# Context attention in a two-layer decoder: from four-head groups in steps to a stream of head pairs

## What is computed

```python
x = x + _L0_xattn_ref(_layernorm(x, axis=-1), ctx_1024, ctx_1024, mask, Wq, bq, Wk, bk, Wv, bv, Wo, bo)

def _L0_xattn_ref(query, key, value, mask, ...):      # 16 heads of 16 features
    q, k, v = proj(query, Wq, bq), proj(key, Wk, bk), proj(value, Wv, bv)
    scores = einsum('bhqd,bhkd->bhqk', q, k) / sqrt(16)
    scores = where(mask == 0, -1e9, scores)            # layer 0 only
    p_attn = softmax(scores, axis=-1)
    return einsum('bhqk,bhkd->bhqd', p_attn, v) ... @ Wo.T + bo
```

## Time and profile before

| what | value |
|---|---|
| median of 3 runs | 2990.66 us |
| lowest and highest | 2989.32 and 2998.60 us |
| profiled execution, its own time | 2986.54 us |
| its span in the profile | 2984.9 us |
| mean granted TensorE clock | 0.886 |

### The profile page before, as it was taken

One profiled execution on the slowest core, in us unless ns is written; L12 is line 12 of the kernel. 1 busy time (PEld: TensorE's weight loads), 2 busy tenths in 40 slices (PEclk: granted clock), 3 DMA queues, 4 the chain that ended last, 5 costly groups with the idle time before them and its releaser, 6 DMA issues. The chain is left out here.

```text
span 2984.9 us, 46600 instructions
## 1 busy us (share of the span) xinstructions
PE 2419.0 (81%) x15980; PEld 1321.5 (44%) x15980; DVE 1588.0 (53%) x2548; ACT 1155.4 (39%) x2075; POOL 984.6 (33%) x836
## 2 busy tenths in 40 slices
PE   3748996575899697799999998858739999847996
PEld 3613434234788475233333332733512222246885
DVE  2758873437233332666666663233658999553223
ACT  1516664242000232344444444224416777711221
POOL 0831003301222111576777776130560000003331
PEclk7959998576999898899999999866869999968998
DMA  3442212432564576122222221543451121024555
GB/s 110 100 89 59 59 38 67 80 72 90 168 211 159 180 195 188 51 77 83 86 77 84 82 78 42 155 73 71 109 102 55 31 57 34 8 76 154 197 195 175
DMA packets 250865, 299.71 MB, mean 100 GB/s; under 512 B 64174, under 2 KB 196948, under 8 KB 250196
## 3 DMA queue, kind: packets, MB, share of 16 engines
q1 hardware_dynamic: 221684, 227.59, 26.2%
q0 software_dynamic: 27104, 68.49, 8.6%
q10 hardware_dynamic: 1920, 1.57, 0.3%
HBM read 205.49 MB, written 91.25 MB: 99 GB/s over the span
## 5 line engine op out<-in xcount | busy, mean ns | idle before, releaser
L1749 ACT ACTIVATE a_probs<-a_cols 128x512 f32<-128x512 f32 (+3 forms) x896 | 445.2, 549 | 239.1 <-PE a_cols L1680 162.1
L1770 DVE TENSOR_REDUCE a_mxw<-a_rows 128x2 f32<-128x1024 f32 (+1 forms) x448 | 475.4, 1099 | 70.6 <-PE a_rows L1638 42.3
L2196 DVE TENSOR_REDUCE a_mxw<-a_rows 128x2 f32<-128x1024 f32 x256 | 313.3, 1224 | 208.3 <-PE a_rows L2034 206.6
L2174 ACT ACTIVATE a_probs<-a_cols 128x1024 f32<-128x1024 f32 x256 | 261.9, 1025 | 266.7 <-PE a_cols L2063 249.6
L2015 POOL TENSOR_TENSOR a_sums<-a_sums,a_probs 128x1024 f32<-128x1024 f32 x128 | 309.6, 2419 | 100.3 <-ACT a_probs L2174 87.1
L1680 PE MATMUL a_cols<-a_qs,a_ks 50*128 50x512 bf16 (+7 forms) x1792 | 275.4, 363 | 17.6 <-DMA a_qs<-a_nparts 11.5
L2450 PE MATMUL e_psU<-e_xT,e_w 128*128 128x256 f32 x1216 | 273.8, 384 | 1.9 <-ACT e_xT L2497 1.2
L2059 PE MATMUL a_cols<-a_qf,a_kf 64*128 64x512 f32 x1024 | 266.5, 598 | 0.0
L522 PE MATMUL t_psP<-t_xT,t_wf 128*128 128x256 f32 x1024 | 236.6, 389 | 36.7 <-ACT t_xT L615 18.1
L1638 PE MATMUL a_rows<-a_ks,a_qs 48*128 48x512 bf16 (+3 forms) x896 | 174.3, 385 | 111.9 <-DMA a_ks<-k_scratch 68.1
L1708 PE MATMUL a_out<-a_probs,a_vs 128*17 128x256 f32 (+4 forms) x3328 | 255.6, 380 | 0.2 <-ACT a_probs L1749 0.2
(11 more groups left out here) (248 smaller groups left out, 3045.7 us busy)
## 6 DMA issues: line engine op xcount, KB each, us to landing
e_w<-in_w SPq DMA_DIRECT2D x69, 512.0 KB
e_w<-in_w SPq DMA_DIRECT2D x30, 1024.0 KB
qk_wide_scratch<-t_f SPq DMA_DIRECT2D x32, 512.0 KB, 2.9
q_scratch<-t_parts POOLq DMA_DIRECT2D x128, 96.0 KB, 2.4
a_qs<-q_scratch SPq DMA_DIRECT2D x96, 128.0 KB
a_qs<-q_scratch SPq DMA_DIRECT2D x168, 64.0 KB, 2.3
a_ks<-k_scratch SPq DMA_DIRECT2D x144, 64.0 KB, 2.6
vw_scratch<-t_v SPq DMA_DIRECT2D x16, 520.0 KB, 7.2
```

Source lines behind the costliest of these rows:

```text
L1749: act.activation(pr[ug % RING][:, 2 * hp + e, c0:512], psC[(2 * at + e) % 3][:, 0:512 - c0], ACT.Exp, scale=scale).then_inc(ex_done, 1)
L1770: dve.tensor_reduce(mxw[w][:, a, :, hp, t % 4:t % 4 + 1], src[:, :, 0:n], AX.X, ALU.max).then_inc(s_free, 1)
L2174: act.activation(pr[i][:], psC[i % 2][:], ACT.Exp, scale=scale).then_inc(ex_done, 1)
L2196: dve.tensor_reduce(mxw[:, j % 2, :, j // 2:j // 2 + 1], psR[:], AX.X, ALU.max).then_inc(s_free, 1)
```

## The change

`attention_stage`, in its `cross=True` form, goes, and `cross_attention_stage` takes its place in a1 and a4; nothing else that a stage computes is changed.

- **Keys and values stay resident.** `context_loads` gives 28 loads (12 of keys per layer, 16 rows x 16 x 77 each, 2 of mask, 1 of values per layer) that SP issues in t0 behind the weights; four memsets in the context stage write ones.
- **Halves of the array.** The six products of parts are two kinds of three ("main" and "rest", 48 rows each). Each kind has two heads of a pair in partitions 0 to 63 and 64 to 127. The maximum is taken over the main kind alone, and the negated maximum has two parts instead of three.
- **A stream of pairs.** 32 steps n of a head pair (512 queries x 2 heads). Rows run `AHEAD = 7` steps ahead of cols in two double banks; cols use three single banks in turn; values come one pair after every second pair.
- **Loads.** Group g's q is 12 loads of 64 KB. SP's order is the place of group g, then the fetch of group g + 2. Group 1's 12 loads are ACT's at the start.
- **Division on VectorE.** A block transpose of the output bank from PSUM, a reciprocal, a multiplication and a block transpose back, in halves between the maxima. TensorE's and ACT's shares in it go.
- **Stores** are 4 x 64 KB per group on POOL, the last group's on SP and ACT. The bias addition moves from the stage's start to the second group on POOL.
- **Zero products.** 20 products on zeros at TensorE's start and one behind each of the first 7 row steps.

```diff
+CROSS_MAIN = ((0, 1), (0, 0), (1, 0))
+CROSS_REST = ((0, 2), (1, 1), (2, 0))
+def zero_products(pe, G, bank, n):
+    for _ in range(n):
+        pe.matmul(bank, G["zerosb"][:, 0:P], G["zerosb"][:], start=True, stop=True)
...
                         for dst, src in loads:
                             sp.dma_start(dst, src).then_inc(w_ld, 16)
+                        for dst, src, sem in later_loads:
+                            sp.dma_start(dst, src).then_inc(sem, 16)
...
+                def place(g):
+                    p = g % 4
+                    sp.wait_ge(mt_done, g + 1)
+                    for e in range(2):
+                        for i in range(2):
+                            row = 64 * e + MAX_ROW + i
+                            sp.dma_start(qs[p][row:row + 1, 0].rearrange("p w m (t q) -> p (w m t) q", q=P),
+                                         nparts[g % 2][TR // 2 * e:TR // 2 * (e + 1), i, :]).then_inc(mld[g % 2], 16)
+                def fetch(g):
+                    if masked and g < 4:
+                        sp.wait_ge(ones_set[g], 2)
+                    wait(sp, st_ready, 8 * (g - 3))
+                    load(sp, g, 0)
+                    load(sp, g, 1)
+                fetch(0)
+                place(0)
+                fetch(2)
+                for g in range(1, NG):
+                    place(g)
+                    if g + 2 < NG:
+                        fetch(g + 2)
...
+                def rows_step(g, j):
+                    p, w, m = g % 4, j // 2, j % 2
+                    dst = psR[at_slot[("step", g, j)] % 2]
+                    if j == 0:
+                        pe.wait_ge(main_ld[p], 16 * n_ld * (g // 4 + 1))
+                    bank_free(("step", g, j))
+                    for t in range(QT // 2):
+                        for e in range(2):
+                            mm = pe.matmul(dst[:, e, t * SC:(t + 1) * SC], qs[p][ROWS_K[e], 0, w, m, t * P:(t + 1) * P],
+                                           keys[ROWS_K[e], 0, g, m, :], start=True, stop=True)
+                    mm.then_inc(s_ready, 1)
...
+                    if n % 4 == 0:
+                        pe.wait_ge(rest_ld[p], 16 * n_ld * (g // 4 + 1))
+                        pe.wait_ge(mld[g % 2], 16 * 4 * (g // 2 + 1))
+                    dst = [psC[(2 * n + e) % 3] for e in range(2)]
+                    for e in range(2):
+                        wait(pe, ex_done, 2 * n + e - 2)
+                        pe.matmul(dst[e][0:SC, :], keys[MAIN_K[e], 0, g, m, :], qs[p][MAIN_K[e], 0, w, m, :],
+                                  start=True, stop=False)
+                    for e in range(2):
+                        pe.matmul(dst[e][0:SC, :], keys[REST_K[e], 1, g, m, :], qs[p][REST_K[e], 1, w, m, :],
+                                  start=False, stop=True).then_inc(st_ready, 1)
...
+                zero_products(pe, G, psO[:], 20)
+                pe.wait_ge(G["ctx_loaded"][layer], n_loads)
+                for n in range(AHEAD):
+                    run(n)
+                    zero_products(pe, G, psO[:], 1)
+                for n in range(NP):
+                    cols_pair(n)
+                    run(n + AHEAD)
+                    if n % 2 == 0 and n:
+                        values(n // 2 - 1)
+                values(NP // 2 - 1)
...
+                for n in range(AHEAD):
+                    run(n)
+                for n in range(NP):
+                    run(n + AHEAD)
+                    if n % 2 == 0 and n:
+                        turn_out(n // 2 - 1)
+                    elif n >= 3:
+                        divide(n // 2 - 1)
+                turn_out(NP // 2 - 1)
+                divide(NP // 2 - 1)
```

More of the change, by code:

```diff
@@ L938, in attention_stage, with cross_attention_stage @@
+def cross_attention_stage(nc, G, tag, *, layer, q, o, masked, n_loads, bias):
     H, hd = 4, 16
-    n_groups = (HEADS // H) * B
-    KT = [(0, SC)] if cross else [(i * P, P) for i in range(S // P)]
-    NK = SC if cross else S
+    NG = (HEADS // H) * B
     QT = S // P
     scale = float(hd) ** -0.5
[L944 to L948, removed]
@@ new lines, in cross_attention_stage @@
+    MAX_ROW = CROSS_MAX + masked
+    ROWS_K = [slice(64 * e, 64 * e + MAX_ROW) for e in range(2)]
+    MAIN_K = [slice(64 * e, 64 * e + MAX_ROW + 2) for e in range(2)]
+    REST_K = [slice(64 * e, 64 * e + CROSS_MAX) for e in range(2)]
+    RING = 3
+    AHEAD = 7
+    TR = H * QT
+    NP = 4 * NG
+    keys, values_of = G["ctx_keys"][layer], G["ctx_values"][layer]
+    slots, at_slot = [], {}
+    for n in range(NP):
+        slots.append(("step", n // 4, n % 4))
+        if n % 4 == 0 and n:
+            slots.append(("turn", n // 4 - 1, 0))
@@ L1313, in _ @@
-                in_thirds(act, n_groups, step)
+                if masked:
+                    act.wait_ge(ones_set[1], 2)
+                load(act, 1, 0)
+                load(act, 1, 1)
+                for n in range(NP):
+                    u, m = n // 2, n % 2
+                    for e in range(2):
+                        act.wait_ge(st_ready, 2 * n + e + 1)
+                        if m == 0 and e == 0:
+                            wait(act, pv_done, u - RING + 1)
+                        act.activation(pr[u % RING][:, 2 * m + e, :], psC[(2 * n + e) % 3][0:SC, :], ACT.Exp, scale=scale
+                                       ).then_inc(ex_done, 1)
@@ L1344, in negate_max @@
[L1344 to L1350 removed]
+                if masked:
+                    for p in range(2):
+                        dve.memset(qs[p][32:64, 0], 1.0).then_inc(ones_set[p], 1)
+                dve.memset(divided[:], 0.0)
@@ L1351, in negate_max, with run, turn_out @@
+                def run(n):
+                    for kind, g, j in slots_of(n):
+                        if kind == "step":
+                            maximum(g, j)
+                        else:
+                            negate_max(g)
+                def turn_out(u):
+                    dve.wait_ge(pv_done, u + 1)
+                    dve.transpose(turned[:].rearrange("p b f -> p (b f)"), psO[:]).then_inc(o_turned, 1)
                     dve.drain()
-                    parts = nparts[p][w]
```

511 lines of the change are left out of this document (143 added, 368 removed).

## The result

| what | before | after |
|---|---|---|
| median | 2991.03 us (5 runs) | 2966.83 us (5 runs) |
| lowest and highest | 2989.32 and 2998.60 us | 2963.57 and 2975.66 us |
| span of the profiled execution | 2984.9 us | 2963.1 us |
| mean granted clock | 0.886 | 0.878 |

The account below looks back on a forecast made before the run. A loop of placing maxima and loading q was to bound each group at 10.6 us; stages of 107.5 us save 36.3 us, less 1 us in t0, giving 2951.2 us profiled and a median of 2955 us, range 2934 to 2978 us.

Parts of the forecast that it names:

- the small terms: Effects outside the two stages: context loads in t0 cost 1 us (bounds 0 and 5), other stages 0.
- start to first T: Stage start until T, when group 0's negated maxima exist: 15 to 17.5 us, taken as 16.
- six periods: Middle of each stage: six group periods of 10.6 us each.
- last T: Step to the last group's negated maxima, without loads: 8.3 us, the second loop less one wait.
- last T to next stage: Stage end: 4.1 us until rows are seen, 8.6 for the last group, 4.9 to the next stage.
- bias addition: POOL's addition, moved to the second group, slows VectorE: 2 us counted, with 0 and 6 as ends.
- the loop of placing and loads: SP places maxima, loads group g+2, then row step, maximum, turn, negation: 10.6 us a group, 10.8 at lower row-step clock.
- the second loop: Period through placed rows, score products, values, turn and negation: 9.4 us at upper, about 11.4 at lower clock (2965 us).
- Loads late: First rival: main q loads land after 4.3 us, period 12.6 us, 2979 us; chance 0.17.
- VectorE's loop: Second rival: loads quicker than in a5, VectorE sets the period at 9.5 us, 2942 us; chance 0.19.
- Clock and loads together: Third rival: falling clock plus late loads use up the gain, period 12.9 to 14.4 us, 2982 to 3000 us; chance 0.06.
- Slower: Fourth rival: SP's queue pushes the period over 14.3 us; at 15 us it would be 3012 us; chance 0.04.

Follow-up runs that it names:

- one_zero: Changed kernel with 1 zero product in place of 27: median 2965.82 us, ratio 0.9911.
- place_split: bias_start with two of the four rows of maxima issued on POOL's queue from group 2 on: median 2948.89 us, ratio 0.9853.
- ahead6: bias_start with AHEAD = 6 in place of 7: median 2972.19 us, ratio 0.9928.
- loads_late: Changed kernel with SP waiting in t0 for the weights to land before issuing the 28 context loads: median 2966.92 us, ratio 0.9909.
- before_again: The kernel before, unchanged and profiled a second time: median 2997.94 us, ratio 1.0012.
- a1_only: Changed kernel with the old stage back in a4 and its 13 context loads left out: median 2977.91 us, ratio 0.9936.
- bias_start: Changed kernel with POOL's bias addition back at the stage's start, behind a drain: median 2959.28 us, ratio 0.9889.
- best: place_split and loads_late together: median 2948.26 us, ratio 0.9843.
- zeros_loop: best with two more zero products ahead of every set of value products: median 2973.90 us, ratio 0.9932.

## Why the prediction was right, and where it was off

**Direction and size.** 2966.8 us lies in the range of 2934 to 2978 us; the gain was 24 us where 36 were forecast. The two stages by themselves saved 20.9 + 12.8 = 33.8 us of the first profile of before, 36.9 us of the mean of both. So the sum of 36.3 us was about right for the stages, but that is in part luck: the loop that was to set the period was not the one that set it in the last groups, and the terms below miss by up to 5 us in both directions. Most of the 12 us between 2955 us and the median lie elsewhere, see the small terms.

**The terms of the sum**, by the rows above:

| term | forecast | a1 | a4 |
|---|---|---|---|
| start to first T | 16 | 13.5 | 13.1 |
| six periods | 63.6 | 60.0 | 66.8 |
| last T | 8.3 | 9.9 | 9.9 |
| last T to next stage | 17.6 | 22.4 | 22.1 |
| bias addition | 2 | in the periods | in the periods |
| sum | 107.5 | 105.8 | 111.8 |

*The start* was counted with the 20 zero products on the path. They took 7.29 us in a1, and one_zero has the first row step at the same place without them: it stands behind its loads.

*The bias addition* was counted at 2 us ("two such operations fall in its 9.3 us"), bounds 0 and 6. Moving it away gives 6.6 us in a4, outside the bounds, and 0.6 us in a1. The row of 2.29 us that I sized it by is one of three in a row, and each took about one of POOL's four operations of 2.3 us:

```profile
550.84 9.28 POOL L138 TENSOR_TENSOR g_X<-g_X,a_bias 128x1024 f32<-128x1024 f32 x4 [3.84 <-DMA a_bias<-in_bo]
...
553.32 2.29 DVE L1355 TENSOR_TENSOR a_nres<-a_neg,a_nparts 32x128 f32<-32x128 f32 x1
555.69 2.21 DVE L1357 CAST a_nparts<-a_nres 32x128 bf16<-32x128 f32 x1
```

What these rows could not tell is that an operation can also be held until the last of the four ends, as in a4.

*The period* was to be the loop of placing and loads, 10.6 us, nearly the same at both clocks. That loop shows only in the first period of a1, 9.2 us; row products waited for q for 2.7 us in the whole stage, all of it in the start and this period. It is shorter than forecast because placing took 2.5 us where a5's took 2.85, and because the turn (565.37 us) runs beside VectorE's maximum (565.48 us), where the sum had one behind the other. What binds later is TensorE's own work, 9.7 us at the lower clock (forecast 10.8), and in the last groups the second loop, 10.8 us (forecast 11.4): place_split shows the first, ahead6 and the rows of group 5 the second. So the 10.0 us are near the forecast's 10.6 us by chance, and the prediction's sentence on the second loop at the lower clock, with its 2965 us, is nearest to what happened. The check that I named, TensorE idle ahead of every fourth row step for a load, failed.

*The end* was counted with products at the higher clock, though the text had named the lower one as likely in a loop that waits. Of the 22.4 us in a1, 4.6 us pass until the rows are seen (forecast 4.1), and then 14.0 us, from 632.13 to 646.13 us, until the last division is done (forecast 8.6). The forecast had one set of value products at 1.05 us in there; three stand in it, at 1.91 us each. Last rows of a1 after, which answer to the earlier trace rows:

```profile
627.51 2.40 SPq L1038 DMA_DIRECT2D a_qs<-a_nparts  x4
...
646.16 0.80 SPq L1059 DMA_DIRECT2D attn_scratch<-a_on  x2
...
649.93 0.41 SPq L411 DMA_DIRECT2D t_wo<-in_wo  x1
```

From the store to the next stage it is 3.8 us, much as before (4.1), where 4.9 us were counted.

**The small terms.** t0 was counted at 1 us of 0 to 5; it cost 2.3 us, all ahead of the first projections, and loads_late gives it back. The other stages were counted at 0, and most of the miss lies here: the two stages save 33.8 us in the first profiles, the span only 21.8 us. a0, t1, t5 and a5 are 2.1, 2.2, 2.0 and 4.1 us longer. For a0, t1 and a5 before_again shows a drift of 1.3 to 2.6 us in the old program too, and over all kernels with a new stage a5 is 417.6 to 422.5 us and t1 60.6 to 63.6 us, around the 418.1 and 420.7, 60.2 and 61.6 us of before. t5 was 107.2 to 110.2 us in all kernels with the resident context, and 105.9 and 106.6 us before; a1_only shows that it is not the new a4. What it is stays open.

**The rivals.** Loads late: no, in a1 loads of q landed 2.1 to 2.7 us after their issue from group 2 on, not over 4 us. VectorE's loop at 9.5 us: no, in place_split's loop it was busy for 7.94 of 10 us and TensorE for all 10. Clock and loads together: the clock fell as described, the loads did not come late. Slower: no; and a period of 15 us makes 3008 us by the prediction's own sum, not 3012. Beside the first of them, priced at 2979 us, stood the Trainium skill ("DMA: Bandwidth & Descriptors", section Bandwidth), by which transfers under 64 KB are dominated by their descriptors. The loads of 64 KB that SP issued alone did not hold the stage up behind its first group, so the rows of these stages do not show that cost. Where it might fit is t0: there the context loads, most of them of 38.5 KB in pieces of 154 bytes (77 keys of 2), delayed the tables by 2.2 us. Whether their size or simply their bytes did it was not tried.

**Signs named.** The start, to the first score products, was 17.2 us in a1 and 16.8 us in a4, alike but under the 20 us named; cols waited for placed rows for 0.3 to 1.6 us behind the first group, as named; t0 and t2 changed by 2.3 and 0.3 us, well under 5 us.

## What to carry to other kernels

When a row shows an operation held up by another engine, count with the whole run of that engine's work as a possible price: a 9 us addition on POOL beside a 0.4 us multiplication on VectorE stalled a pipeline for 7 us, and for 0.6 us in the twin stage. Compute the periods of all loops that close over a group at both levels of the clock before choosing the one that binds; they were 9.2, 9.7 and 10.8 us here, and taking 1.3 us of issue out of the placing made TensorE's own the longest. Take two profiles of the old kernel before reading 3 us in a stage.

## What the runs showed of the hardware

With TensorE busy for 10.00 of every 10 us over 50 us, the granted clock stayed at 0.50 (place_split, and best too), and two zero products of 128x512 per set of values did not change it (zeros_loop). In a5 of the kernel before a loop of half-height products ran at 1.00 with TensorE busy for 96 of 100 us:

```profile
2300.30:2400.30 100.00, 95.96 (x973) 26.45 (x965) 93.70 (x103) 77.27 (x143) 5.93 (x12) 1.00 0.22 61
```

The Trainium skill ("TensorE: Matmul & The Clock Gate", Part 1) says that activity releases the throttle. a5 agrees with that; in a1 the engine that the profile shows as busy without a gap kept the lower level. So from the profile's busy time alone the level could not be told here, and why the two stages differ stays open.

VectorE's multiplication, 0.43 us by itself, took up to 8.79 us while POOL's four additions ran, and negations took 0.27 and 0.28 us while they ran in bias_start.
